# Fused norms, transposed weighted values and a bias moved to VectorE in an eight-stage transformer kernel

## The chip, the cores and the metric

One core of a Trainium2 chip runs the whole kernel. The time is device microseconds from start to end, the median of several runs; lower is better. Beside the runs there is one execution taken by the hardware profiler, from which all rows below come.

## What is computed

The reference keeps a residual `x` of 8 batches x 128 rows x 512 columns and passes it through four layers of an attention and a feed-forward network. Each of the eight adds its result, scaled by a gate, to the residual:

```python
x = x + jnp.tanh(g_xattn[l]) * attention_l(_layernorm(x), ctx)
x = x + jnp.tanh(g_ffn[l]) * ffn_l(_layernorm(x))
```

Five of them are touched by the change. The first feed-forward rounds its three weight matrices to the 16 levels of NF4 (blocks of 64, scaled by the block's largest value) and then computes `silu(x @ w1.T) * (x @ w2.T) @ w3.T`, with 1376 hidden columns. The second attention is a linear attention over the context. The second feed-forward mixes eight low-rank experts per batch:

```python
q = x.mean(axis=1) @ Wq.T                       # one query per batch
coeffs = softmax(q @ lora_keys.T / sqrt(128))   # 8 experts
h = einsum('bsi,eir->bser', x, lora_down)       # rank 64 each
out = x @ W_org.T + einsum('be,bser,ero->bso', coeffs, h, lora_up)
```

The third attention has 16 query heads of 96 columns that share 4 key and value heads, over 128 context and 128 own positions. The third feed-forward is `x @ W_base.T + b_base` and, per row, the two best of eight rank-16 experts.

## The kernel before

The residual stays in SBUF. The eight sublayers are stages, one Python function each: `l0_attention`, `l0_ffn`, `l1_attention`, `l1_ffn`, `l2_attention`, `l2_ffn`, `l3_attention`, `l3_ffn`.
**The norm.** Ahead of each sublayer `layernorm_all` (L108) is a block of its own. `row_stats` (L102) has taken the statistics of each batch when it was updated. The block then makes mean and variance of the 8 batches (DVE, L135 and L137), the reciprocal root by a power (POOL, L170), and normalises 8 batches on DVE (L152, L157 and L163). Where the sublayer wants it transposed, PE transposes each batch (L185, L194) into PSUM and ACT copies it out (L204) to `chip.hall`, which the stages call `h_t`. Only two buffers are there, so that DVE, PE and ACT take turns. The block can be given loads for SP to issue and work for POOL (`prepare`).

**`l0_ffn`** (L678). The weights come in 11 chunks. For each, DVE takes the largest values (L912), divides by them (L924), and compares with the 15 boundaries: each comparison is a `side`, 128x1536 in f16 (L932). PE sums the sides, each multiplied with a diagonal matrix that carries the step of its level (`level`, L776: three matmuls). The 15 diagonals are written by POOL at L737, in the norm's block. For chunk 0, PE waits for all of them at once. The main block follows, with the gate and up products (L795) and the down products (L847), and DVE's update of `x` (L979).

**`l1_attention`** (L1038). After its norm, SP issues here the loads for `l2_attention` (`l2_attention_loads`, L1015). The last is the output weight `wo`, one transfer of 3 MB.

**`l1_ffn`** (L1233). A loop over four pairs of batches. POOL copies a batch of `h_t` (L1278), PE makes the down products (L1290, 16 matmuls of 128 columns), the query (L1295) and the scores (L1301), DVE and ACT make the softmax, DVE scales the down products by it (`hl`), and PE sums base and up products (L1306, L1309, four matmuls of 512 columns each).

**`l2_attention`** (L1459). It runs batch by batch in one cycle, in which PE works for batch `b` and prepares `b + 1`:

```python
scores_t(b, 0); output(b - 1, range(6, OT)); scores_t(b, 1)     # PE, cycle(b), shortened
queries(n, 0); weighted_values(b, 0); queries(n, 1); weighted_values(b, 1)
queries(n, 2); weighted_values(b, 2); keys(n, 0); weighted_values(b, 3)
keys(n, 1); keys(n, 2); values(n, 0); o_transposed(b, 0); o_transposed(b, 1); scores(n, 0)
o_transposed(b, 2); values(n, 1); scores(n, 1); output(b, range(0, 3)); maxima_as_rows(n); output(b, range(3, 6))
```

`scores_t` (L1624, L1627) makes the scores transposed, in `a_ps_st`; ACT's `exponential` (L1732) turns them into probabilities, `a_p_t_ctx` and `a_p_t_lat`. `weighted_values(b, r)` (L1640) takes the 128x128 probabilities of one head as the stationary operand and 97 columns as the moving one: the 96 values and a column of ones, which gives the sum. DVE takes the reciprocal of the sums and multiplies (L1815, L1817), PE transposes the result (L1651), ACT copies it (L1737), and `output` (L1661) multiplies it with `wo` in 12 tiles. On DVE the same cycle rounds the weights of the last feed-forward (`rounding`).

**`l2_ffn`** (L1882). Pairs of batches again. Per batch PE sums four base matmuls (L1957), one that adds the bias (`ones` of 1x128 by the bias, L1958), a transpose (L1960) and the experts' product (L1962).

Of the kernel before, what the change touches and what calls it, by code (L numbers as in the profile page):

```python
# [16 lines left out]
ALU = mybir.AluOpType  # L17
# [3 lines left out]
P = 128  # L21
NB = 8
# [85 lines left out]
def layernorm_all(chip, tag, transposed, loads=None, rms=False, prepare=None, scratch=None):  # L108
# [103 lines left out]
    if transposed:  # L212
        chip.ln_counts["transposed"] += NB
        chip.ln_counts["stored"] += NB

# [462 lines left out]
def l0_ffn(chip):  # L678

    nc, a = chip.nc, chip.args
# [12 lines left out]
    with ExitStack() as ctx:  # L694
# [40 lines left out]
        def diagonals(pool):  # L735
            for k in range(LEVELS):
# [3 lines left out]
        layernorm_all(chip, "f0", transposed=True, loads=first_loads, prepare=diagonals,  # L740
                      scratch=q[:, :].rearrange("p (u n) -> p u n", u=2))
# [6 lines left out]
        with nc.Block() as block:  # L748
            @block.sync
            def _(sp):  # L750
                with sp.Fori(1, MT // 2) as i:
# [10 lines left out]
                sp.dma_start(wch[:, 0, 2 * D:2 * D + LAST3], w3[:, m * D:FLAT]).then_inc(s_wl[0], 16)  # L762

            @block.tensor
            def _(pe):
                pe.sem_inc(s_used, RING)
                pe.sem_inc(s_u, 2)
                pe.wait_ge(s_dg, LEVELS)

                def level(m, k, first=False):  # L770
                    after(pe, s_sg, m * LEVELS + (k + 1))
# [53 lines left out]

                for k in range(LEVELS):
                    level(0, k, first=True)
                transposed(0, 0, first=True)
                transposed(0, 1)
                step(0, 0)  # L830
# [21 lines left out]
            def _(act):  # L852
# [38 lines left out]

                w3_scaled(0, 0)
# [14 lines left out]
            def _(dve):  # L907
# [54 lines left out]

                maxima(0, 0, 48)
                normalized(0, 0, first=True)
                sides(0, 0, range(LEVELS))
# [11 lines left out]
                for b in range(NB):  # L977
# [3 lines left out]
                    row_stats(chip, dve, b, s_x, b + 1)  # L981

# [32 lines left out]
def l2_attention_loads(chip):  # L1015
# [12 lines left out]
    return loads + [(wv, a["l2_wv"], landed), (wo, a["l2_wo"], landed)]  # L1028
# [3 lines left out]
L2_LOADS = KT * U2 * (1 + HEADS2 // KV2) + 2  # L1032
# [5 lines left out]
def l1_attention(chip):  # L1038
# [3 lines left out]
    layernorm_all(chip, "a1", transposed=False, loads=l1_ffn_loads(chip))  # L1042
# [190 lines left out]
def l1_ffn(chip):  # L1233

# [3 lines left out]
    worg, down, up, wq, keys = l1_ffn_weights(chip)  # L1240
    with ExitStack() as ctx:
# [3 lines left out]
        psc, phl, pout = ps("ps_score", [P, 2, D]), ps("ps_hl", [P, 2, D]), ps("ps_out", [P, 2, D])  # L1245
        ones = sb("ones", [P, P])
        hs = sb("h_b", [P, 2, KT, P])
        hm = sb("h_sum", [P, 2, KT])
        qb = sb("q_bcast", [P, 2, P])
        nmx = sb("neg_max", [P, 2, 1])  # L1250
        e8 = sb("exp", [P, 2, E1])
        es = sb("exp_sum", [P, 2, 1])
        er = sb("exp_rec", [P, 2, 1])
        cc = sb("coeff", [P, 2, KT])
        hl = sb("hl", [P, 2, KT, P])
# [203 lines left out]
def l2_attention(chip):  # L1459
# [10 lines left out]
    with ExitStack() as ctx:  # L1470
# [69 lines left out]
        with nc.Block() as block:  # L1540
# [23 lines left out]
            def _(pe):  # L1564
# [66 lines left out]
                def weighted_values(b, r, first=False):  # L1631
                    if r == 0:
                        after(pe, s_v, b * 2 + 2)
# [1156 lines left out]
```

## Time and profile before

| what | value |
|---|---|
| median of 3 runs | 1694.49 us (1693.63 to 1696.26) |
| the profiled execution | 1687.38 us |
| its span, first to last instruction | 1685.6 us |
| its mean granted TensorE clock | 0.92 |
| PE busy | 1444.7 us (86%) |
| DVE busy | 1021.8 us (61%) |
| ACT busy | 356.8 us (21%) |
| POOL busy | 62.8 us (4%) |

The stages stand one behind the other, so the profile is read stage by stage: the time of a row is the start of an instruction or of a run of like instructions, counted from the start of the span, and the figure behind it is how long they took. A bracket says how long the engine had been idle and which operation ended the wait. The shares of the table are means over eight stages with different limits.

### The profile page before, as it was taken

Reading aid. Unit: us, or ns where it says so; the run is one execution under the profiler, and the core shown is the slowest. Engines: PE = TensorE matmul, PEld = TensorE weight load, DVE = VectorE, ACT = ScalarE, POOL = GpSimd, SP = SyncE. Lnnn points to the kernel's source line nnn. Section 1 sums busy time; section 2 is a strip of 40 time slices with the busy share of each in tenths; the row PEclk is TensorE's granted clock in tenths of the full one; section 3 lists DMA queues with packets and bytes.
Section 4 is the critical chain, followed back from the end, with each engine's and each line's share of the span. In section 5 each row is a group of like instructions: output and inputs, shape, how many; then the busy total and the mean of one; then the engine's idle time right before and its main releaser. Section 6 shows DMA issues by size and latency. Waiting matters only on the chain. (4 is left out here: it accounts for less than half of the span.)

```text
span 1685.6 us, 26597 instructions
## 1 busy us (share of the span) xinstructions
PE 1444.7 (86%) x8875; PEld 891.3 (53%) x8875; DVE 1021.8 (61%) x1652; ACT 356.8 (21%) x705; POOL 62.8 (4%) x100
## 2 busy tenths in 40 slices
PE   2989758999999966997999999999787789996575
PEld 1666623444444435665667777666443656652232
DVE  6577569778871137233566667666334256767886
ACT  1333321111113012101112121211111223332221
POOL 2000020000000000000000000000004000000000
PEclk9999858999999988898999999999698899998887
DMA  5000011011100037000000000000120000000000
GB/s 208 2 0 0 1 38 38 20 38 37 33 0 1 0 98 171 0 0 6 27 22 18 21 26 26 20 26 21 66 40 1 1 1 1 0 0 1 12 19 19
DMA packets 52311, 44.56 MB, mean 26 GB/s; under 512 B 38497, under 2 KB 38689, under 8 KB 51362
## 3 DMA queue, kind: packets, MB, share of 16 engines
q1 hardware_dynamic: 52258, 43.85, 8.8%
q8 instruction: 33, 0.54, 0.1%
q14 instruction: 20, 0.16, 0.0%
HBM read 41.74 MB, written 2.10 MB: 26 GB/s over the span
## 5 line engine op out<-in xcount | busy, mean ns | idle before, releaser
L932 DVE TENSOR_SCALAR f_side<-f_chunk 128x1536 f16<-128x1536 f32 x165 | 148.1, 955 | 46.1 <-PE f_sum L776 45.0
L776 PE MATMUL f_sum<-f_side,f_diag 128*128 128x512 f16 x495 | 122.2, 389 | 9.6 <-DVE f_side L932 8.1
L776 PEld LDWEIGHTS f_sum<-f_side,f_diag 128*128 128x128 f16 x495 | 47.9, 100 | 92.0 <-issue 45.0
L1573 PE MATMUL a_ps_b<-h_all,weights_a 128*128 (+1 forms) x768 | 92.1, 280 | 1.3 <-PEq L124 1.3
L1573 PEld LDWEIGHTS a_ps_b<-h_all,weights_a 128*128 128x128 f32 x768 | 89.1, 195 | 5.9 <-issue 5.9
L1661 PE MATMUL a_ps_y<-weights_a,a_o_t 128*128 128x512 f32 x192 | 89.3, 613 | 2.7 <-DVE a_v_ones L1793 2.0
L795 PE MATMUL f_gate<-h_all,f_w_t 128*128 128x512 f32 (+1 forms) x176 | 87.6, 598 | 0.0
L795 PE MATMUL f_up<-h_all,f_w_t 128*128 128x512 f32 (+1 forms) x176 | 79.6, 592 | 0.0
L847 PE MATMUL f_sum<-weights_a 128*128 128x512 f32 (+1 forms) x176 | 75.7, 592 | 0.0
L453 PE MATMUL a_o<-weights_a 128*128 128x128 f32 x512 | 70.1, 287 | 0.0
L453 PEld LDWEIGHTS a_o<-weights_a 128*128 128x128 f32 x512 | 62.7, 196 | 7.4 <-issue 3.5
L2237 PE MATMUL a_ps_a<-h_all,weights_a 128*128 (+1 forms) x512 | 64.1, 286 | 2.5 <-DVE a_sel L2482 2.5
L2237 PEld LDWEIGHTS a_ps_a<-h_all,weights_a 128*128 128x128 f32 x512 | 61.3, 200 | 9.2 <-issue 9.2
L2508 DVE TENSOR_REDUCE a_neg_max<-a_ps_a 128x8 f32<-128x1024 f32 x32 | 39.2, 1225 | 37.2 <-PE a_ps_a L2267 37.2
L1661 PEld LDWEIGHTS a_ps_y<-weights_a,a_o_t 128*128 128x128 f32 x192 | 35.6, 195 | 46.1 <-issue 45.9
L598 DVE TENSOR_REDUCE a_neg_max<-a_sa 128x8 f32<-128x1024 f32 x32 | 39.2, 1225 | 34.3 <-PE a_sa L416 34.0
L389 PE MATMUL a_proj<-h_all,a_wqk 128*128 (+1 forms) x64 | 36.6, 685 | 25.6 <-DVE a_neg_lo L564 24.1
L847 PEld LDWEIGHTS f_sum<-weights_a 128*128 128x128 f32 (+1 forms) x176 | 33.4, 190 | 42.2 <-issue 42.2
L1640 PE MATMUL a_ps_o<-a_v_ones,a_p_t_ctx 128*128 128x97 f32 x256 | 51.6, 285 | 4.0 <-DVE a_o L1817 3.2
L2416 ACT ACTIVATE a_p_t<-a_ps_st 128x512 f32<-128x512 f32 x64 | 34.8, 596 | 87.7 <-PE a_ps_st L2293 87.6
L170 POOL TENSOR_TENSOR ln_rstd<-ln_meanvar,ln_minus_half 128x8 f32<-128x8 f32 x7 | 11.6, 1652 | 1095.2 <-DVE ln_meanvar L137 1095.2
L795 PEld LDWEIGHTS f_up<-h_all,f_w_t 128*128 128x128 f32 (+1 forms) x176 | 32.8, 188 | 37.0 <-issue 35.6
(334 smaller groups left out, 2677.1 us busy)
## 6 DMA issues: line engine op xcount, KB each, us to landing
f_chunk<-in_l_w SPq DMA_DIRECT2D x30, 256.0 KB, 3.0
weights_a<-in_l_wgu SPq DMA_DIRECT2D x16, 232.0 KB
weights_a<-in_l_wq SPq DMA_DIRECT2D x48, 64.0 KB, 2.4
weights_a<-in_l_wo SPq DMA_DIRECT2D x1, 3072.0 KB, 11.6
weights_a<-in_l_wd SPq DMA_DIRECT2D x16, 192.0 KB, 3.1
x_res<-in_x SPq DMA_DIRECT2D x1, 2048.0 KB, 8.1
ctx_nat<-in_ctx SPq DMA_DIRECT2D x1, 2048.0 KB, 11.2
a_mask<-in_mask SPq DMA_DIRECT2D x1, 2048.0 KB, 15.7
```

The source lines that it names most:

```text
L389: nc.tensor.matmul(pproj[:, g % 2, :], wqk[:, g, :], h_n[:, bass.ds(b, 1), :].rearrange("p a n -> p (a n)"), start=True, stop=True).then_i ...
L453: mm = nc.tensor.matmul(po[:, c], vpad[:, s, n, k * P:(k + 1) * P], pt[:, k % 4, c], start=(k == 0 and n == 0), stop=(k == H0 - 1), skip_g ...
L598: nc.vector.tensor_reduce(to, psa[:, :, :].rearrange("p e (n j) -> p e n j", n=WN), AX.X, ALU.max, negate=True).then_inc(s_max, 1)
L776: mm = nc.tensor.matmul(psum[:, j, :], diag[:, k, :], side[:, k % RING, j * D:(j + 1) * D], start=(k == 0), stop=(k == LEVELS - 1), skip_g ...
L795: mm = nc.tensor.matmul((pg, pu)[w][0:r, g, :], wt[:, u, w, k, 0:r], h_t[:, k, g * D:(g + 1) * D], start=(k == 0), stop=(k == KT - 1), ski ...
L847: mm = nc.tensor.matmul(psum[:, i % 2, :], hid[0:r, t, i * P:(i + 1) * P], w3t[0:r, t, :], start=(t == 0), stop=(t == MT - 1))
L932: nc.vector.tensor_scalar(side[:, k % RING, :], wch[:, u, :], bounds[k], steps[k][0], ALU.is_le if k < ZERO else ALU.is_gt, ALU.mult).then ...
L1573: mm = nc.tensor.matmul(pb[:, u % 2, g * P:(g + 1) * P], wq_of(k, u, g), h_t[:, k, bass.ds(b * P, P)], start=(k == 0), stop=(k == KT - 1))
L1640: mm = nc.tensor.matmul(po[:, g * (HD2 + 1):(g + 1) * (HD2 + 1)], p, v[:, part, r, :], start=(part == 0), stop=(part == 1))
L1661: mm = nc.tensor.matmul(py[:, :], ot[:, t, :], wo[:, t, :], start=(t == 0), stop=(t == OT - 1))
L2237: mm = nc.tensor.matmul(pa[:, u // QG, (u % QG) * P:(u % QG + 1) * P], wq[:, k, u * P:(u + 1) * P], hb(b)(k), start=(k == 0), stop=(k == K ...
L2508: nc.vector.tensor_reduce(to, pa[:, :, :].rearrange("p e (i j) -> p e i j", i=QG), AX.X, ALU.max, negate=True).then_inc(s_max, 1)
```

## The change

A new class, `NextNorm`, takes the place of several norm blocks. Its parts are mean, variance (DVE), the power (POOL, for one batch) and the normalising pass (DVE), and a stage calls them batch by batch.

**A. `l0_ffn`.** Its norm block is gone. The norm's first parts stand ahead of chunk 0's maxima on DVE; six of eight normalising passes stand between the first sides. PE transposes each batch between the levels, into the banks of the gate product, and ACT copies it. Each level of chunk 0 waits for its own diagonal. At the end of the stage DVE normalises each batch for `l1_attention` behind its update. The five loads of `l1_ffn`'s weights are issued in this stage.

```diff
-        layernorm_all(chip, "f0", transposed=True, loads=first_loads, prepare=diagonals,
-                      scratch=q[:, :].rearrange("p (u n) -> p u n", u=2))
+        first_norm = NextNorm(chip, sem, "first")
...
+            @block.gpsimd
+            def _(pool):
+                pool.wait_ge(first_norm.s_mv, 2 * NB)
+                nc.gpsimd.tensor_tensor(chip.ln_rstd[:], chip.ln_mv[:, :, 1], chip.ln_mhalf[:], ALU.pow)\
+                  .then_inc(first_norm.s_rstd, NB)
+                diagonals(pool)
+                for b in range(NB):
+                    norm.rstd(pool, b)
...
                 def level(m, k, first=False):
+                    if first:
+                        pe.wait_ge(s_dg, k + 1)
...
+                first_norm.meanvars(dve)
+                for b in range(2):
+                    input_normalized(b)
                 maxima(0, 0, 48)
                 normalized(0, 0, first=True)
-                sides(0, 0, range(LEVELS))
+                for k in range(LEVELS):
+                    sides(0, 0, range(k, k + 1))
+                    if k < NB - 2:
+                        input_normalized(k + 2)
...
                     row_stats(chip, dve, b, s_x, b + 1)
+                    norm.meanvar(dve, b)
+                    norm.normalized(dve, b, chip.hall[:, b * D:(b + 1) * D])
```

On PE, at the start of `l0_ffn`, the order before was this (`ln_psf` is the norm's PSUM, `f_diag` the diagonals):

```order
L185 MATMUL ln_psf<-ident,f_q 128x128 x8
L188 UNCONDITIONAL_BRANCH
L188 ISA
L32 REGISTER_ALU
L194 MATMUL ln_psf<-ident,f_q 128x128 x4
L32 REGISTER_ALU
L194 MATMUL ln_psf<-ident,f_q 128x128 x4
L188 REGISTER_ALU
L188 COMPARE_AND_BRANCH
L124 UNCONDITIONAL_BRANCH
L764 UNCONDITIONAL_BRANCH
L776 MATMUL f_sum<-f_side,f_diag 128x512 x45
```

Now the same place on PE reads:

```order
L831 MATMUL f_gate<-ident,f_q 128x128 x8
L843 MATMUL f_sum<-f_side,f_diag 128x512 x3
L831 MATMUL f_gate<-ident,f_q 128x128 x4
L843 MATMUL f_sum<-f_side,f_diag 128x512 x3
L831 MATMUL f_gate<-ident,f_q 128x128 x4
L843 MATMUL f_sum<-f_side,f_diag 128x512 x3
```

This alternates until six transposed batches stand between seven levels; the other eight levels follow, and no block ends in between.

**B. `l1_attention`.** Its norm block is gone, and `wo` is laid out anew, in 16 transfers:

```diff
-    layernorm_all(chip, "a1", transposed=False, loads=l1_ffn_loads(chip))
...
-    return loads + [(wv, a["l2_wv"], landed), (wo, a["l2_wo"], landed)]
+    for r in range(KV2):
+        for m in range(4):
...
+            loads.append((to[:, m], a["l2_wo"][32 * m:32 * m + 32, U2 * r:U2 * r + U2, :], landed))
```

**C. `l1_ffn`.** Its own norm block stays, the loop over pairs is written out straight. The down products take 512 columns at a time (four batches). Queries, scores and softmax are made once for all batches. POOL's copies are gone. Behind each update DVE normalises the batch for `l2_attention`, and PE transposes it after the next batch's output:

```diff
+                downs(0, (0, 1))
+                queries()
+                downs(0, (2,))
+                scores()
+                downs(0, (3,))
...
+                for b in range(NB):
+                    if b == HALF:
+                        downs(1, range(KT))
+                    outputs(b)
+                    if b:
+                        transposed(b - 1)
+                transposed(NB - 1)
```

**D. `l2_attention`.** Its norm block is gone. The weighted values turn round: 32 columns of ones or of values are stationary, in four column groups beside one another (one for each key head), and 512 columns of probabilities move. The result comes out transposed, so PE's 12 transposes and ACT's copies are gone. DVE takes one reciprocal of 128x512 and multiplies three times:

```diff
+                    for out, of in [(po, lambda part, r: ones32[:, :])] + \
+                            [(pst[:, u, :], lambda part, r, u=u: v[:, part, r, 32 * u:32 * u + 32]) for u in range(U)]:
+                        for part, p in enumerate((pt0, pt1)):
+                            for r in range(KV2):
+                                mm = nc.tensor.matmul(out[row(r), :], of(part, r), p[:, r, :], start=(part == 0),
+                                                      stop=(part == 1), skip_group_check=True)
...
+                def reciprocals(b):
+                    after(dve, s_pv, b * 4 + 1)
+                    nc.vector.reciprocal(rec[:, :], po[:, :]).then_inc(s_rec, 1)
...
-                            weighted_values(b, r)
-                        o_transposed(b, 0, (s_ot, b * 3))
-                        o_transposed(b, 1)
-                        o_transposed(b, 2, (s_ot, b * 3 + 1))
+                        weighted_values(b)
                         output(b, range(OT), (s_x, b))
```

On PE, in a cycle of `l2_attention`, the place of the weighted values before (two of the four heads groups; `a_ps_b` from `h_all` are the queries of the next batch):

```order
L1573 MATMUL a_ps_b<-h_all,weights_a 128x128 x16
L1640 MATMUL a_ps_o<-a_v_ones,a_p_t_ctx 128x97
L1640 MATMUL a_ps_o<-a_v_ones,a_p_t_lat 128x97
L1640 MATMUL a_ps_o<-a_v_ones,a_p_t_ctx 128x97
L1640 MATMUL a_ps_o<-a_v_ones,a_p_t_lat 128x97
L1640 MATMUL a_ps_o<-a_v_ones,a_p_t_ctx 128x97
L1640 MATMUL a_ps_o<-a_v_ones,a_p_t_lat 128x97
L1640 MATMUL a_ps_o<-a_v_ones,a_p_t_ctx 128x97
L1640 MATMUL a_ps_o<-a_v_ones,a_p_t_lat 128x97
L1573 MATMUL a_ps_b<-h_all,weights_a 128x128 x16
```

Now:

```order
L1708 MATMUL a_ps_b<-h_all,weights_a 128x128 x16
L1777 MATMUL a_ps_o<-a_p_t_ctx,a_ones 32x512 x4
L1777 MATMUL a_ps_o<-a_p_t_lat,a_ones 32x512 x4
L1777 MATMUL a_ps_st<-a_p_t_ctx,a_v 32x512 x4
L1777 MATMUL a_ps_st<-a_p_t_lat,a_v 32x512 x4
L1777 MATMUL a_ps_st<-a_p_t_ctx,a_v 32x512 x4
L1777 MATMUL a_ps_st<-a_p_t_lat,a_v 32x512 x4
L1777 MATMUL a_ps_st<-a_p_t_ctx,a_v 32x512 x4
L1777 MATMUL a_ps_st<-a_p_t_lat,a_v 32x512 x4
L1708 MATMUL a_ps_b<-h_all,weights_a 128x128 x16
L1726 MATMUL a_ps_y<-weights_a,a_ctx_b 128x384 x4
```

All weighted values of a batch stand together, after the first queries of the next; its first values (`a_ctx_b`) come earlier. All four ACT buffers of `a_p_t_lat` are there, so no exponential waits for PE to free one. The outputs are cut 0 to 2, 3 to 5, 6 and 7, and 8 to 11 (before: 0 to 2, 3 to 5, 6 to 11); the scores of the next batch wait for the three multiplications, since they write the same PSUM.

**E. `l2_ffn`.** The bias matmul is gone. The bias is loaded to all 128 partitions, scaled by the gate once, and added to `x` on DVE ahead of each batch's update:

```diff
-                        nc.tensor.matmul(pout[:, u, :], ones[:, :], bias, start=False, stop=False)
...
+                        nc.vector.tensor_tensor(chip.x_at(b), chip.x_at(b), bias, ALU.add).then_inc(s_xb, 1)
+                    for u in range(2):
+                        b = pair * 2 + u
+                        after(dve, s_xb, b + 1)
```

## Rows read from the trace of the kernel before

**Rows 1.** Windows, a cycle and the end of `l2_attention`: us; busy by engine; clock; DMA

```profile
core 0: us, PE busy (x) PEld busy (x) DVE busy (x) ACT busy (x) POOL busy (x), PEclk, DMA share, GB/s
971.00:1019.50 48.50, 48.17 (x368) 35.15 (x364) 33.26 (x63) 9.90 (x19) 0.00 (x0) 1.00 0.08 23
1177.00:1198.00 21.00, 15.46 (x80) 13.79 (x76) 13.89 (x29) 4.04 (x7) 0.00 (x0) 0.63 0.00 1
```

**Rows 2.** Timeline, start of `l0_ffn`, DVE, POOL and the SP queue: start, duration

```profile
234.24 2.70 SPq L129 DMA_DIRECT2D f_chunk<-in_l_w  x6
...
236.90 1.08 DVE L157 TENSOR_SCALAR f_q<-x_res,ln_meanvar,ln_rstd 128x512 f32<-128x512 f32 x2 [1.77 <-POOL ln_rstd L170]
...
236.96 10.35 POOL L737 TENSOR_SCALAR f_diag<-ident 128x128 f16<-128x128 f32 x15
...
247.76 1.75 DVE L912 TENSOR_REDUCE f_absmax<-f_chunk 128x24 f32<-128x1536 f32 x1 [2.67 <-PEq L124]
...
251.90 2.70 DVE L932 TENSOR_SCALAR f_side<-f_chunk 128x1536 f16<-128x1536 f32 x3
```

**Rows 3.** Tile `f_chunk`, the six chunk transfers, 230 to 262 us

```profile
DMA to landing us min/median/max: 2.7/4.3/5.3
```

**Rows 4.** Timeline, `l0_ffn`'s end into `l1_attention`, DVE and the SP queue

```profile
614.74 0.75 DVE L979 SCALAR_TENSOR_TENSOR x_res<-f_sum,tanh_g,x_res 128x512 f32<-128x512 f32 x1 [7.97 <-PE f_sum L847]
...
624.75 0.39 SPq L1080 DMA_DIRECT2D weights_a<-in_l_wk  x1
...
658.66 0.43 SPq L1080 DMA_DIRECT2D weights_a<-in_l_wo  x1
...
668.03 0.69 DVE L105 BATCH_NORM_STATS2 ln_stats<-x_res 128x6 f32<-128x512 f32 x1
```

**Rows 5.** Lines by form, POOL's power for one batch, elsewhere: busy, mean ns

```profile
L2118 POOL TENSOR_TENSOR ln_rstd<-ln_meanvar,ln_minus_half 128x1 f32 x8 | 4.4, 544 | 229.8 <-DVE ln_meanvar L2112 229.8
```

**Rows 6.** Timeline, `l1_ffn` and the start of `l2_attention`, POOL and PE

```profile
683.16 0.20 POOL L1273 MEMSET f_ones<- 128x128 f32 x1 [11.06 <-POOLq L124]
...
773.44 3.60 PE L1306 MATMUL f_ps_out<-weights_b,f_h_b 128*128 128x512 f32 x8
776.88 3.60 PE L1309 MATMUL f_ps_out<-weights_b,f_hl 128*128 128x512 f32 x8
...
796.53 3.76 PE L1573 MATMUL a_ps_b<-h_all,weights_a 128*128 128x128 f32 x17 [1.25 <-PEq L124]
```

**Rows 7.** Timeline, PE, one cycle of `l2_attention`, 1017 to 1069 us

```profile
1034.51 0.36 PE L1640 MATMUL a_ps_o<-a_v_ones,a_p_t_ctx 128*128 128x97 f32 x2
...
1036.27 3.76 PE L1573 MATMUL a_ps_b<-h_all,weights_a 128*128 x32
...
1056.75 1.04 PE L1651 MATMUL a_ps_b<-ident,a_o 128*128 128x128 f32 x8
...
1058.48 0.66 PE L1651 MATMUL a_ps_b<-ident,a_o 128*128 128x128 f32 x4
...
1062.82 2.81 PE L1661 MATMUL a_ps_y<-weights_a,a_o_t 128*128 128x512 f32 x6 [0.33 <-DVE a_v_ones L1793]
```

**Rows 8.** Timeline, ACT, the same cycle, its first four exponentials

```profile
1022.66 2.06 ACT L1732 ACTIVATE a_p_t_ctx<-a_ps_st 128x512 f32<-128x512 f32 x4 [11.58 <-PE a_ps_st L1627]
```

**Rows 9.** Timeline, PE, `l3_attention`: 128x32 column groups of 512 columns

```profile
1400.87 1.06 PE L2304 MATMUL a_ps_o<-a_p_t,a_v_pad 128*32 128x512 f32 x8
1401.75 1.04 PE L2304 MATMUL a_ps_den<-a_p_t,a_ones 128*32 128x512 f32 x8
```

**Rows 10.** Lines by form, DVE's reciprocal of 128x512 in `l3_attention`

```profile
L2520 DVE RECIPROCAL a_rec<-a_ps_den 128x512 f32<-128x512 f32 x8 | 26.8, 3356 | 2.9 <-PE a_ps_den L2304 2.9
```

**Rows 11.** Timeline, PE, the last cycle of `l2_attention`

```profile
1165.77 2.86 PE L1624 MATMUL a_ps_st<-a_q_t,a_k_t 32*128 32x512 f32 x24
...
1198.08 12.88 PE L1661 MATMUL a_ps_y<-weights_a,a_o_t 128*128 128x512 f32 x24 [0.77 <-ACT a_o_t L1737]
```

**Rows 12.** Timeline, PE, `l2_ffn`, around one bias matmul

```profile
1251.59 1.12 PE L1958 MATMUL f_ps_out<-f_bias,f_ones 1*128 1x512 f32 x2
1252.64 0.33 PE L1960 MATMUL f_ps_tr<-ident,f_weighted 128*128 128x128 f32 x1
```

More of the change, by code:

```diff
@@ L1273, in _ @@
                 nc.gpsimd.memset(ones[:], 1.0).then_inc(s_c, 1)
-                with pool.Fori(0, NB // 2) as pair:
-                    for u in range(2):
-                        b = pair * 2 + u
-                        after(pool, s_y, b + 1)
-                        nc.gpsimd.tensor_copy(hs[:, u, :, :], h_t[:, :, bass.ds(b * P, P)]).then_inc(s_hs, 1)
+                for b in range(NB):
+                    norm.rstd(pool, b)
             @block.tensor
@@ new lines, in _, with downs @@
+                pe.wait_ge(s_c, 1)
+                def downs(part, tiles):
+                    if part and tiles[0] == 0:
+                        pe.wait_ge(s_hl, HALF)
+                    for t in tiles:
+                        for k in range(KT):
+                            mm = nc.tensor.matmul(phl[:, t, :], down[:, k, t * P:(t + 1) * P],
+                                                  h_t[:, k, part * D:(part + 1) * D], start=(k == 0), stop=(k == KT - 1))
+                        mm.then_inc(s_hp, 1)
@@ new lines, in queries, with scores @@
+                def queries():
+                    pe.wait_ge(s_hm, 1)
+                    for k in range(KT):
+                        mm = nc.tensor.matmul(pq, wq[:, k, :], hm[:, k, :], start=(k == 0), stop=(k == KT - 1))
+                    mm.then_inc(s_q, 1)
+                def scores():
+                    pe.wait_ge(s_qk, 1)
+                    nc.tensor.matmul(pscore, ones[:], qk[:, :, :].rearrange("p b e -> p (b e)"), start=True, stop=True)\
+                      .then_inc(s_sc, 1)
@@ L1313, in _ @@
+                for b in range(NB):
+                    if b == HALF:
+                        downs(1, range(KT))
+                    outputs(b)
+                    if b:
+                        transposed(b - 1)
+                transposed(NB - 1)
             @block.scalar
             def _(act):
[L1315 to L1320 removed]
+                act.wait_ge(s_sh, 1)
@@ L1364 @@
+                for part in range(2):
+                    for b in range(part * HALF, part * HALF + HALF):
+                        scaled(b)
+                    for b in range(part * HALF, part * HALF + HALF):
+                        updated(b)
 MXB = 32
@@ L1561, in _ @@
                         raw_loads(j, p)
+            @block.gpsimd
+            def _(pool):
+                constants(pool)
             @block.tensor
```

393 lines of the change are left out of this document (212 added, 181 removed).

## The prediction

> **What bounds the kernel now.** I read the shares first, then windows by stage, since a share over eight stages says nothing of one, and then the timelines at the places that the diff touches. In `l2_attention` PE is the bound: in a window of 48.50 us, about one cycle, it is busy for 48.17 at full granted clock, and DVE for 33.26 [rows 1]. So what PE no longer does there comes off the time, as long as DVE, which gets more, stays below. At the two ends of a stage it is otherwise: there the chain is norm, barrier, first product, and every engine but one waits. At the start of `l0_ffn` DVE makes its first maximum at 247.76, after a norm and 2.67 us of waiting for the block's end [rows 2]. Between `l0_ffn`'s last update at 614.74 and the first load of the next stage at 624.75 lie 10 us of norm and barriers [rows 4], between `l1_ffn`'s last product (776.88 + 3.60 = 780.48) and the first queries 16.05 [rows 6]. The last cycle of `l2_attention` has no next batch to cover its waits: it lasts from 1165.77 to 1198.08 + 12.88 = 1210.96, 45.2 us, with a granted clock of 0.63 in the middle [rows 1, 11].
>
> The sum is made against the profiled execution, 1687.4 us, which lies 7.1 under the median of 1694.5; I take the same difference off the median.
>
> **A, the first feed-forward: 4.0.** Before, sides begin at 251.90, which is 4.14 after the maxima begin [rows 2]. Now the maxima need two normalising passes, which ended at 236.90 + 1.08 = 237.98, and the chunk. Its third transfer is issued by about 235.6 (half of six that take 2.70 from 234.24) and lands 4.3 later [rows 2, 3], at 239.9. Sides can begin at 244.0, 7.9 earlier. Against it stand the six other passes, 6 x 0.55 = 3.3 on DVE, which paces the levels here. Transposes by PE and copies by ACT lie beside sides of 0.9 us each. For a slow first stretch of PE I take off another 0.6; 4.0 remain. The diagonals do not hold the levels: they come every 10.35 / 15 = 0.69 from 236.96 on [rows 2], and a side takes longer. Bounds: 6.4, if the chunk lands with the second pass and nothing else is lost. Below, DVE and POOL may get in each other's way: with sides from 244.0 there are some 5 diagonals left, and with the passes and maxima ahead of them up to 10, at 0.69 each; that would make it -3. But two passes took 1.08 while diagonals were being written, so I stay with 4.0.
>
> The Trainium skill (SBUF — State Buffer, "SBUF: two separate sides") speaks against this part: VectorE and GpSimd share a port pair that one operation holds alone, and the other blocks until it is done. By that, the 10 diagonals would cost up to 6.9 and A would come out below nothing; the two passes beside diagonals, 0.54 each [rows 2], don't show such a block.
>
> **B, the second attention's norm: 5.8.** The last update starts at 614.74 and takes 0.75. Behind it now come statistics (0.69, [rows 4]), mean and root's argument (some 0.3 with their waits), POOL's power (0.54, [rows 5]) and one pass (0.55): with the waits between them 618.0, and with a barrier of 0.9, 618.9 instead of 624.75. Bounds 4.7 to 6.0. SP gets 15 more issues of 0.43 for `wo`, 6.5 in all. Their cover: the old last one ends at 659.09, and the stage's last update has its statistics until 668.72 [rows 4], so 9.6 us are free. They would cost if an issue took over 0.64.
>
> **C, the second feed-forward: 17.8.** Four matmuls of 512 columns take 3.44 from start to start, 0.86 each [rows 6]. PE now has 32 for the down products (27.5) and 64 for the outputs (55.0), small products of 1.2, and seven times four transposes at 0.12 to 0.13 (3.6); for a slow start I add 1.5. From 683.4, when the block starts [rows 6], that is 88.8 and ends at 772.2, 8.3 earlier. DVE's work for a batch (scaling, update, norm: about 3.5) hides behind 6.9 of output; if it did not, each of six batches would pay the rest. Of the end, 16.05 before, there stay update, norm (3.5 as in B without its barrier), four transposes at half clock and a copy (2.0) and the barrier (0.9): 6.4, so 9.6 less. I take 17.8 for both; bounds 14 (if softmax delays the first outputs by its whole chain) and 19.
>
> **D, the third attention: 22.3.** Per cycle goes 4 x 1.76 = 7.04 of weighted values (1034.51 to 1036.27 for one of four), 12 transposes of 1.04 + 0.66 busy, about 1.5 without overlap, and the wait of 0.33 [rows 7]. There come 8 groups of four matmuls. `l3_attention` has the same form: one to the next takes 1401.75 - 1400.87 = 0.88 [rows 9], so 7.04. Left are 1.8, of which I keep 1.5 for changes of operand and tiling: 7 cycles, 10.5. The new wait is for DVE: reciprocal 3.36 [rows 10] and three multiplications of 0.7 take the place of four small pairs, 2.5 more in 33.3 of 48.5. By its order they are done some 22 us into a cycle, and PE needs them at about 38, after the queries, keys and values of the next batch. Bounds 0 (the wait takes all) and 12.6.
>
> The last cycle now is: transposed scores and four output tiles, 3.0 + 3.6 + 3.0; four exponentials that nothing covers, 2.06 [rows 8] and 0.3; 7.1 of weighted values, behind which the reciprocal hides; 1.0 for the last multiplication; 12 output tiles, 12.88 as before [rows 11]. That is 33.0, 12.2 less. Bounds: 14.4 at full clock throughout. With the clock at half from the exponentials on, 14.2 and 21.4 replace 7.1 and 12.88: 48.6, a loss of 3.4. I take 12.2, since PE has one wait of 2.4 now where it had one before each of four groups. POOL's constants, no longer beside a norm, cost 0.4 at the start.
>
> The Trainium skill (TensorEngine Tiling (Array Packing), "Key Properties") says that a change of tiling mode drains TensorE. Its cost is bounded by a row: a group of 1.06, followed after 0.88 [rows 9], leaves at most 0.18 hidden, twice a batch, 2.9 in all.
>
> **E, the third feed-forward's bias: 7.6.** From the bias matmul to the next instruction are 1.05 [rows 12]; eight are 8.4. I take 0.95 each, since a transpose that follows another row of products may start a little dearer. DVE gets 0.69 per batch, ahead of an update that waits for PE. Bounds 8.4, and 0 if DVE ends each pair.
>
> **Sum:** 4.0 + 5.8 + 17.8 + 22.3 + 7.6 = 57.5. The profiled execution would take 1629.9, the median 1637.0.
>
> **The rivals.** *Tilings drain* (0.10): each batch enters and leaves the column groups, at 0.18 each: 1640. For it: the group's 1.06 against 0.88; against it: the next group, without a change, shows 1.04 too. The skill's page on tiling has this rule.
>
> *The first norm does not hide* (0.12): what the change says of A does not come about; passes between the sides delay PE's levels as much as the norm did, A is 0, and 1641. For it: DVE paces this stretch, and the passes are on it still. Against: the wait of 2.67 and the ping-pong of DVE, PE and ACT are gone in any case.
>
> *DVE ends the cycle* (0.08): reciprocal and rounding push the maxima of the next batch behind PE, and the 10.5 of the steady cycles go: 1647.5. For it: the maxima already stand close ahead of PE's last tiles, which waited 0.33 for DVE [rows 7]. Against: 15 us of DVE's cycle are free.
>
> *Half clock in the last cycle* (0.10): 12.2 turns into -3.4, and 1652.6. For it: the granted clock was 0.63 between 1177 and 1198 [rows 1], after waits of PE; against: fewer waits.
>
> *The other side, slower* (0.02): the four column groups run one behind another. A group of four then takes 4 x 0.88 = 3.5, 2.64 more, 64 times: 169, and 1806. It decides from 57.5 / 64 = 0.9 more per group, about 1.8, on. Against it: 0.88 in `l3_attention` for the same form [rows 9]. Only that operands sit elsewhere speaks for it.
>
> **How the numbers follow.** The forecast has 0.58. A measurement of this kernel can tell about 0.2%, 3.4 us, from no change; all cases but the last are over 30 us faster, so faster has 0.97, slower 0.02, and 0.01 is for several bounds met at once. Downwards the bounds of A, C, D and E reach 57.5 + 2.4 + 1.2 + 4.3 + 0.8, 1628; with 2.6 for the scatter of the runs, 1625. Upwards the range takes in all rivals but the last: 1652.
>
> **What would show it.** In the changed kernel sides of chunk 0 should begin near 244, and the gate product some 4 us earlier against that stage's start. `l0_ffn`'s last update should be followed by the next stage's first load within 4.2. `l1_ffn` should last some 89 us and the next stage's queries follow its last product by 6 to 7. A group of four at the weighted values should take 0.88; the transposed scores of the next batch should follow after 47.2 or so, and PE should not wait for the multiplications. The last cycle should last 33. Groups over 1.0, a wait of PE for DVE in the cycle, or a granted clock near 0.6 over the last outputs would prove the sum wrong.

## The result, and the profile after

| what | before | changed |
|---|---|---|
| median of 3 runs | 1694.49 us | 1632.45 us (1631.99 to 1637.58) |
| ratio, 95% interval | | 0.9641 [0.961, 0.9673] |
| the profiled execution, its span | 1687.38, 1685.6 | 1637.58, 1635.9 |

The forecast was 1637.0 between 1625 and 1652, by 57.5 us. The medians differ by 62.0, the profiled executions by 49.8, and a second measurement, further down, gives a ratio of 0.9685 [0.9653, 0.9718], 52.9 us. So the totals alone can't judge a sum of 57.5. The stages can. I cut both traces at the same events: the statistics that begin a norm, the second maximum of `l0_ffn`, the last update and the first load behind it, the first and the last product of a stage.

| stretch | before | changed | less by | forecast |
|---|---|---|---|---|
| start to `l0_ffn`'s statistics (`l0_attention`) | 234.28 | 241.28 | -7.0 | 0 |
| A: to chunk 1's maxima | 31.45 | 26.48 | 5.0 | 4.0 |
| the other chunks, to the last update | 349.01 | 347.42 | 1.6 | 0 |
| B: to the next stage's first load | 10.01 | 3.99 | 6.0 | 5.8 |
| `l1_attention` | 44.78 | 47.04 | -2.3 | 0 |
| `l1_ffn`'s norm block | 13.63 | 12.89 | 0.7 | 0 |
| C: `l1_ffn`'s body and the way to the next queries | 97.32 + 16.05 | 88.40 + 5.89 | 19.1 | 17.8 |
| D: `l2_attention` | 414.43 | 393.08 | 21.4 | 22.3 |
| E: `l2_ffn`, to the next norm's statistics | 82.57 | 76.65 | 5.9 | 7.6 |
| the rest | 392.07 | 392.78 | -0.7 | 0 |

The five parts give 57.4 together. What the profiled executions differ from that lies in stretches for which the sum had nothing, above all in the first, which has no edit. The windows view of the changed kernel shows it (us, busy time by engine, granted clock, DMA); in the kernel before the same window has a granted clock of 0.87.

```profile
20.00:60.00 40.00, 28.68 (x199) 16.99 (x200) 20.64 (x41) 9.77 (x16) 0.00 (x0) 0.74 0.15 58
941.00:988.00 47.00, 46.72 (x353) 28.66 (x351) 35.36 (x59) 8.02 (x16) 0.00 (x0) 1.00 0.08 23
1130.00:1166.00 36.00, 32.88 (x189) 13.15 (x187) 30.46 (x50) 4.13 (x8) 0.00 (x0) 1.00 0.07 18
```

The second and third line are a cycle and the last cycle of `l2_attention`, to set beside [rows 1]: PE is still the bound, DVE has 35.36 instead of 33.26, and the last cycle now runs at full granted clock.

**A and B.** The timeline of the changed kernel at `l0_ffn`'s start and end, DVE, POOL and the SP queue (start, duration; beside [rows 2] and [rows 4]):

```profile
241.15 2.70 SPq L795 DMA_DIRECT2D f_chunk<-in_l_w  x6
...
241.28 0.64 DVE L239 BATCH_NORM_AGGREGATE ln_meanvar<-ln_stats 128x2 f32<-128x6 f32 x8 [1.00 <-PEq L87]
...
244.11 15.60 POOL L777 TENSOR_SCALAR f_diag<-ident 128x128 f16<-128x128 f32 x15
...
247.28 1.75 DVE L988 TENSOR_REDUCE f_absmax<-f_chunk 128x24 f32<-128x1536 f32 x1 [2.14 <-DMA f_chunk<-in_l_w]
...
251.40 0.96 DVE L1008 TENSOR_SCALAR f_side<-f_chunk 128x1536 f16<-128x1536 f32 x1
252.28 0.54 DVE L252 TENSOR_SCALAR f_q<-x_res,ln_meanvar,ln_rstd 128x512 f32<-128x512 f32 x1
252.74 1.04 DVE L1008 TENSOR_SCALAR f_side<-f_chunk 128x1536 f16<-128x1536 f32 x1
...
267.76 1.74 DVE L988 TENSOR_REDUCE f_absmax<-f_chunk 128x24 f32<-128x1536 f32 x1
...
615.18 0.75 DVE L1066 SCALAR_TENSOR_TENSOR x_res<-f_sum,tanh_g,x_res 128x512 f32<-128x512 f32 x1 [6.35 <-PE f_sum L919]
...
619.17 0.38 SPq L1173 DMA_DIRECT2D weights_a<-in_l_wk  x1
```

The maxima wait for the chunk, as the sum had it. Sides begin 10.12 after the statistics, 7.5 earlier than before (7.9 forecast). A pass between two sides costs 0.46 from start to start, not 0.55. The diagonals take 15.60 instead of 10.35, but not evenly. The same row in three parts, with DVE's division of the chunk:

```profile
244.11 5.66 POOL L777 TENSOR_SCALAR f_diag<-ident 128x128 f16<-128x128 f32 x9
249.61 1.76 DVE L1000 TENSOR_TENSOR f_chunk<-f_chunk,f_rec 128x1536 f32<-128x1536 f32 x1
249.85 2.65 POOL L777 TENSOR_SCALAR f_diag<-ident 128x128 f16<-128x128 f32 x1
252.59 7.13 POOL L777 TENSOR_SCALAR f_diag<-ident 128x128 f16<-128x128 f32 x5
```

Nine diagonals come every 0.64. The tenth starts beside the division and takes 2.65. The last five stand beside sides and come every 1.4, as often as a side with its pass.

**C and D.** PE in the changed kernel: the end of `l1_ffn` (beside [rows 6]), then one cycle of `l2_attention` (beside [rows 7]) and the last one (beside [rows 11]).

```profile
763.90 3.60 PE L1410 MATMUL f_ps_out<-weights_b,f_hl 128*128 128x512 f32 x8
...
770.75 0.66 PE L1425 MATMUL f_ps_norm<-ident,f_next_h 128*128 128x128 f32 x4 [2.82 <-DVE f_next_h L252]
773.39 13.32 PE L1708 MATMUL a_ps_b<-h_all,weights_a 128*128 128x128 f32 x96 [1.98 <-POOL a_ones L1664]
...
945.30 2.86 PE L1759 MATMUL a_ps_st<-a_q_t,a_k_t 32*128 32x512 f32 x24
...
958.71 1.06 PE L1777 MATMUL a_ps_o<-a_p_t_ctx,a_ones 128*32 128x512 f32 x8
959.59 1.04 PE L1777 MATMUL a_ps_o<-a_p_t_lat,a_ones 128*32 128x512 f32 x8
960.45 1.04 PE L1777 MATMUL a_ps_st<-a_p_t_ctx,a_v 128*32 128x512 f32 x8
...
964.74 1.04 PE L1777 MATMUL a_ps_st<-a_p_t_lat,a_v 128*32 128x512 f32 x8
965.71 3.84 PE L1708 MATMUL a_ps_b<-h_all,weights_a 128*128 x32
...
984.65 2.81 PE L1788 MATMUL a_ps_y<-weights_a,a_o_t 128*128 128x512 f32 x6 [0.24 <-DVE a_v L1898]
987.39 0.83 PE L1741 MATMUL a_ps_st<-a_k,a_q 32*128 32x256 bf16 x24
988.16 2.84 PE L1788 MATMUL a_ps_y<-weights_a,a_o_t 128*128 128x512 f32 x6
...
991.18 1.88 PE L1788 MATMUL a_ps_y<-weights_a,a_o_t 128*128 128x512 f32 x4
992.99 2.86 PE L1759 MATMUL a_ps_st<-a_q_t,a_k_t 32*128 32x512 f32 x24
...
1136.07 2.86 PE L1759 MATMUL a_ps_st<-a_q_t,a_k_t 32*128 32x512 f32 x24
...
1147.96 1.07 PE L1777 MATMUL a_ps_o<-a_p_t_ctx,a_ones 128*32 128x512 f32 x8 [2.18 <-issue]
...
1155.93 10.54 PE L1788 MATMUL a_ps_y<-weights_a,a_o_t 128*128 128x512 f32 x24 [0.90 <-DVE a_o_t L1925]
```

A group of four column groups takes 0.86, as long as a single matmul of 512 columns ([rows 6], 3.44 for four), so they run beside one another. A cycle is 992.99 - 945.30 = 47.69; before, three cycles took 146.28 (from 1019.48 to the last one's 1165.77), 48.76 each. The last cycle takes 1166.47 - 1136.07 = 30.4 instead of 45.2.

**E.** The changed kernel in `l2_ffn`, from all engines (beside [rows 12]):

```profile
1172.00 8.55 SPq L129 DMA_DIRECT2D weights_a<-in_l_wv  x1
...
1186.79 3.96 PE L2066 MATMUL f_ps_ra<-f_w_ra,f_h_b 128*128 128x136 f32 x16 [5.29 <-POOL f_h_b L2053]
...
1201.31 2.34 PE L2066 MATMUL f_ps_ra<-f_w_ra,f_h_b 128*128 128x136 f32 x16
1203.48 3.60 PE L2073 MATMUL f_ps_out<-f_w_base,f_h_b 128*128 128x512 f32 x8
1206.92 0.27 PE L2075 MATMUL f_ps_tr<-ident,f_weighted 128*128 128x128 f32 x1
1207.72 1.10 PE L2077 MATMUL f_ps_out<-f_w_b,f_weighted_t 128*128 128x512 f32 x2 [0.53 <-ACT f_weighted_t L2089]
...
1213.83 2.34 PE L2066 MATMUL f_ps_ra<-f_w_ra,f_h_b 128*128 128x136 f32 x16
...
1227.36 14.95 POOL L2186 TENSOR_SCALAR weights_a<-f_raw_queries,weights_a 128x256 f32<-128x256 f32 x16
...
1239.35 0.75 DVE L2140 SCALAR_TENSOR_TENSOR x_res<-f_ps_out,tanh_g,x_res 128x512 f32 x1 [1.56 <-PE f_ps_out L2077]
...
1243.12 0.64 DVE L135 BATCH_NORM_AGGREGATE ln_meanvar<-ln_stats 128x2 f32<-128x6 f32 x8 [2.08 <-PEq L87]
```

A pair of batches takes 1213.83 - 1201.31 = 12.52; before it took 14.92, so a batch is 1.20 shorter. Beside the bias matmul of [rows 12] stood, before:

```profile
1248.07 3.60 PE L1957 MATMUL f_ps_out<-f_w_base,f_h_b 128*128 128x512 f32 x8
...
1253.50 1.10 PE L1962 MATMUL f_ps_out<-f_w_b,f_weighted_t 128*128 128x512 f32 x2 [0.53 <-ACT f_weighted_t L1974]
```

So 1.05 of the 1.20 is the matmul itself; the base products ahead of it took 3.52 and take 3.44 now, and the transpose took 0.86 to the next product and takes 0.80. From the first product to the last update that is 52.56 instead of 62.05, so 9.5 less. But the first product comes 2.3 later after the norm's statistics than before, and from the last update to the next statistics pass 3.77 instead of 2.47: POOL works until 1242.31.

### The profile page after: what moved, and what is told of

It reads as the page before. It is cut to its first block and busy times, and to the rows that moved or that the text cites. A ratio compares the mean times of both kernels' runs of the same rounds, so it can differ in the third digit from the quotient of the medians.

```text
span 1635.9 us, 25134 instructions
## 1 busy us (share of the span) xinstructions
PE 1409.3 (86%) x8501; PEld 811.8 (50%) x8501; DVE 1042.4 (64%) x1603; ACT 338.8 (21%) x666; POOL 69.3 (4%) x105
## 5 line engine op out<-in xcount | busy, mean ns | idle before, releaser
L492 PE MATMUL a_o<-weights_a 128*128 128x128 f32 x512 | 74.6, 300 | 0.0
L492 PEld LDWEIGHTS a_o<-weights_a 128*128 128x128 f32 x512 | 67.1, 208 | 8.1 <-issue 4.5
L1759 PE MATMUL a_ps_st<-a_q_t,a_k_t 32*128 32x512 f32 x384 | 48.7, 623 | 1.6 <-DVE a_neg_max_block L1912 0.8
L1906 DVE TENSOR_REDUCE a_neg_max<-a_ps_st 128x4 f32<-128x1024 f32 x32 | 37.7, 1220 | 12.0 <-PE a_ps_st L1741 12.0
```

The costliest lines, as they stand in the source:

```text
L492: mm = nc.tensor.matmul(po[:, c], vpad[:, s, n, k * P:(k + 1) * P], pt[:, k % 4, c], start=(k == 0 and n == 0), stop=(k == H0 - 1), skip_g ...
L1759: nc.tensor.matmul(pst[:, r, :], kt[row(r), u, part * P:(part + 1) * P], qt[row(r), u, :], start=(u == 0), stop=False, skip_group_check=True)
```

## The experiments

**The parts, one at a time.** Four runs undo one part of the changed kernel and keep the others: A (norm and diagonals in a block of their own again), B, C, D; a fifth undoes E. Their edits are the diffs of the change, read backwards (C's run also makes the third attention's norm a block again, D's loads `wo` in one transfer again); of each the line that stands for it, shortened:

```diff
+        layernorm_all(chip, "f0", transposed=True, loads=first_loads, prepare=diagonals,
+                      scratch=q[:, :].rearrange("p (u n) -> p u n", u=2))
```

> The changed kernel with the first feed-forward's norm as a block of its own ahead of chunk 0, with POOL's diagonals in it; the rest as changed. Theory (part A is worth what the stage shows, 4.97): chunk 1's maxima begin 31.45 after the stage's first statistics instead of 26.48, and 1637.4 in all. Rival (the moved norm gave nothing, and the stage's earlier end came from later chunks): the maxima come as early, 1632.4.

```diff
-                    norm.normalized(dve, b, chip.hall[:, b * D:(b + 1) * D])
...
+    layernorm_all(chip, "a1", transposed=False)
```

> The changed kernel with the second attention's norm as a block again; the 16 transfers of the output weight stay. Theory (part B is worth 6.0): from the first feed-forward's last update to the next stage's first load 10.0 instead of 4.0, 1638.4 in all. Rival (the 16 transfers cost what the norm gives: the second attention took 2.3 longer in the changed kernel): then the stage from its first load to the next norm's statistics stays at 47.0 here too, and it is the 16 transfers that make it so; if it falls to 44.8 in this run or differs from run to run, it is the granted clock.

```diff
-                downs(0, (0, 1))
-                queries()
...
+                        nc.gpsimd.tensor_copy(hs[:, u, :, :], h_t[:, :, bass.ds(b * P, P)]).then_inc(s_hs, 1)
...
+        layernorm_all(chip, "a2", transposed=True, prepare=constants, scratch=ot[:, 0:2, :])
```

> The changed kernel with the second feed-forward as before (pairs of batches, POOL's copies, 128 columns) and with the third attention's norm as a block. Theory (part C is worth 19.1: 8.9 in the products, 10.2 at the end): from the stage's first memset to its last product 97.3 instead of 88.4, from there to the next queries 16.05 instead of 5.9, and 1651.5 in all. Rival (the 512-column products alone matter, the norm at the end hides elsewhere): 9 us, 1641.

```diff
-                        weighted_values(b)
+                        for r in range(KV2):
+                            weighted_values(b, r)
+                        o_transposed(b, 0, (s_ot, b * 3))
```

> The changed kernel with the third attention's products as before (97 columns move, transposes, four small reciprocals per batch, the output weight in one transfer); its norm stays with the second feed-forward. Theory (part D is worth the 21.35 that the stage shows: 7 cycles of 1.07, and 14.8 in the last one): a cycle of 48.76, the last one 45.2 with a granted clock of 0.6 in it, 1653.8 in all. Rival (half of the last cycle's 14.8 was the clock that one execution happened to have): the last cycle 33 to 38 and 1643 to 1647.

```diff
+                        nc.tensor.matmul(pout[:, u, :], ones[:, :], bias, start=False, stop=False)
```

> The changed kernel with the third feed-forward as it was before: the bias is a matmul again and one 2 KB transfer. Theory (the part is worth what the stage shows: products 9.5 us shorter, but 1.8 given back while SP issues the stage's loads, and 1.3 while POOL finishes): from the last update of the third attention to the statistics of the next norm 82.5 instead of 76.6, and 1638.4 us in all. Rival (PE's sum alone counts, the waits at both ends of the stage are chance of one execution): 9.5 longer, 1642. Both say that SP's issue of the values' weights takes 6.9 again, not 8.55, if it is the bias's 128 copies that hold it up; if it stays at 8.5, the copies have nothing to do with it.

| part undone | its stretch, changed | in this run | worth | all, median (4 runs) |
|---|---|---|---|---|
| A | 26.48 | 32.29 | 5.8 | 1641.31 |
| B | 3.99 | 10.53 | 6.5 | 1640.65 |
| C | 88.40 + 5.89 | 97.51 + 15.92 | 19.1 | 1650.14 |
| D | 393.08 | 415.05 | 22.0 | 1661.33 |
| E | 76.65 | 82.22 | 5.6 | 1641.96 |

Each stretch returns to within 0.9 of what it was before, so each gain belongs to its part, and the rivals fall; the sum is 59.0. How far a stretch scatters by itself is seen in the traces that leave its part in place: A's is 25.0 to 26.5 in nine traces, B's 3.95 to 3.99 in ten, C's 92.6 to 94.9 and D's 393.1 to 395.6 in ten (the longest is the run that undoes C), E's 76.4 to 77.3 in seven. A's scatters because the first maxima begin 4.1 to 6.0 after the statistics, with the landing of the chunk, and the later chunks make up for it: from the statistics to the stage's last update the nine take 373.5 to 374.6, the run that undoes A 380.1, the kernel before 380.5. Over the stage A is worth 5.5 to 6.6.

The medians of all lie 1.4 to 7.5 us off the totals that the theories gave, too much to read a part of 6 from them. E's median, 9.5 above the changed kernel's, would have spoken for the rival; by its ratio to the kernel before, 0.9701 against 0.9641 and 0.9685, E reads as anything from 3 to 10. D's last cycle takes 45.42 again, and the windows view of that run shows the clock of its middle:

```profile
1155.00:1176.00 21.00, 15.13 (x84) 13.36 (x76) 14.00 (x29) 4.00 (x7) 0.00 (x0) 0.64 0.00 1
```

So the low clock returns with the old order of waits, and is a part of D's worth. In the run without B, with the 16 transfers, `l1_attention` took 47.5; in the run without D, with one transfer, 47.1; in the runs without A, C and E 45.9 to 46.1. Neither the transfers nor the norm set it. It goes with the granted clock of the stage: 0.79 in the six traces with 47.0 to 47.5, 0.80 to 0.82 in the five with 45.9 to 46.1, 0.83 in the kernel before, with 44.8. E's run also shows SP's issue of the values' weights without the bias's 128 copies ahead of it:

```profile
1163.57 6.96 SPq L129 DMA_DIRECT2D weights_a<-in_l_wv  x1
```

**The wait for the diagonals.** One line:

```diff
-                        pe.wait_ge(s_dg, k + 1)
+                        pe.wait_ge(s_dg, LEVELS)
```

> The changed kernel, where each level of chunk 0 waits for all 15 diagonals, as before. Theory (POOL writes a diagonal in 1.04 now instead of 0.69, since DVE works beside it, and is done 18.4 us after the stage's statistics begin, 8 us behind the first side; the three side buffers then stop DVE): the maxima of chunk 1 come 3 to 5 later than 26.5 us after the start, and 1636 in all, so most of what the moved norm gained hangs on the wait being cut up. Rival (DVE's stop lets POOL finish sooner and PE catches up, since its levels are shorter than DVE's sides): under 1 us, 1633.

Chunk 1's maxima came 31.66 after the statistics instead of 26.48, and 1640.22 in all. The whole gain of A goes, 5.2 where 3 to 5 were expected. The timeline, POOL, PE and DVE:

```profile
239.00 13.01 POOL L777 TENSOR_SCALAR f_diag<-ident 128x128 f16<-128x128 f32 x15
...
252.06 1.46 PE L843 MATMUL f_sum<-f_side,f_diag 128*128 128x512 f16 x3 [10.47 <-POOL f_diag L777]
...
254.42 0.55 DVE L252 TENSOR_SCALAR f_q<-x_res,ln_meanvar,ln_rstd 128x512 f32<-128x512 f32 x1 [4.98 <-PE f_gate L831]
```

DVE stops for 4.98, though not for a side's buffer as expected: its next pass waits for a transpose that stands behind the first level in PE's order.

**The bias's place.** The transfer is issued last, with a semaphore of its own:

```diff
+            + [(bias, chip.args["l2_bias"].rearrange("a n -> (a n)").partition_broadcast(P), s_bias)])
...
-                dve.wait_ge(chip.s_l2f, 16 * 4)
+                dve.wait_ge(s_bias, 16)
```

> The changed kernel with the bias's transfer issued behind all others of that block, on a semaphore of its own, so that the products don't wait for it. Theory (the 128 copies ahead of the values' weights hold SP's issues up, and the block ends with SP): the values' weights are issued in about 6.9 instead of 8.55, the stage's first product comes about 1.7 earlier after the norm's statistics, 1630.7 in all. Rival (SP's long issue is paced by the transfers of the values' weights themselves): 8.5 stays, and no change, 1632.4.

SP's long issue fell to 7.18 and the norm block ended 1.5 earlier. But the stage took 77.85, not less than 76.65, and 1632.01 in all. The timeline shows the wait that took its place, which neither theory had:

```profile
1167.23 7.18 SPq L129 DMA_DIRECT2D weights_a<-in_l_wv  x1
...
1178.91 0.42 SPq L129 DMA_DIRECT2D f_bias<-in_l_bias  x1
...
1185.54 0.49 DVE L2098 TENSOR_SCALAR f_bias<-f_bias,tanh_g 128x512 f32<-128x512 f32 x1 [5.42 <-DMA f_bias<-in_l_bias]
...
1189.72 0.30 PE L2076 MATMUL f_ps_tr<-ident,f_weighted 128*128 128x128 f32 x1 [1.83 <-DVE f_weighted L2128]
```

DVE scales the bias ahead of all its work, so it waited for the transfer, and PE for DVE.

**Three ends of stages.** As the run before, with POOL's layout of the next queries cut in four portions and PE's waits for POOL's constants put ahead of their first use.

```diff
-                l3_queries_laid_out(chip, pool, raw_queries)
+                    l3_queries_laid_out(chip, pool, raw_queries, pair)
...
                 pe.wait_ge(chip.s_l2a, 16 * L2_LOADS)
-                pe.wait_ge(s_c, 3)
...
                 values(0, 0)
+                pe.wait_ge(s_c, 3)
                 scores(0, 0)
```

> As the run with the bias last, and two more: POOL lays out the next attention's queries in four portions between its copies instead of behind the last (14.95 us that end 1.3 after DVE), and PE waits for POOL's constants only ahead of their first use (it waited 1.40 for ones in the second feed-forward and 1.98 for ones in the third attention, of which part is the barrier). Theory (the stage ends with POOL, and the starts with POOL's constants): the third feed-forward ends 1.3 earlier, the two starts 0.3 to 0.8 each earlier; with the bias's 1.7 some 4 in all, 1628.4. Rival (the portions delay the copies that PE needs, and the block's barrier was the wait at the starts): the copies come up to 2 late per pair, no gain in all, 1631 or more.

The portions did what they should: 2.48 from the last update to the next statistics instead of 3.77, and 76.52 for the stage, with the bias's wait still in it. The constants gave nothing: the queries began 0.5 earlier after the last product (5.37), and `l2_attention` took 0.6 longer (393.68). In all 1633.39 (6 runs), no change.

**The loads later.** The bias stays in its place; SP issues the fourth attention's loads in the main block, POOL's portions follow the copies from the second pair on.

```diff
-            + l3_attention_loads(chip, raw_queries))
...
+            @block.sync
+            def _(sp):
+                for dst, src, landed in l3_attention_loads(chip, raw_queries):
+                    sp.dma_start(dst, src).then_inc(landed, 16)
```

> The changed kernel, where SP issues the fourth attention's loads in the third feed-forward's main block instead of its norm block (the bias stays where the change has it), and POOL lays out the queries in four portions behind its copies from the second pair on. Theory (the norm block ends with SP's issues, 3 us behind the last copy of the norm, and the main block with POOL, 1.3 behind DVE): the stage's first memset comes 2.3 earlier after the norm's statistics (14.2 instead of 16.5), the next norm's statistics 1.3 earlier after the last update, the stage takes 73.0 instead of 76.65, 1628.8 in all. Rival (the loads then land too late for POOL, or their transfers hold up the products): 76 or more, and no change in all.

> The changed kernel itself once more, beside the run with the loads later. Theory (its stages after the first are the same from run to run, and the first attention takes 234 to 241 with no edit in it, by the granted clock of its first part: 0.87 against 0.74 between 20 and 60 us): stages within 1 of those of the first profile, apart from the first attention, the second (45.9 to 47.5) and the part behind the third feed-forward (390 to 398); a time from 1629 to 1638. Rival (the new code itself sets the slower clock at the start): 241 here too, and in every other run that has the changed first feed-forward; four of those runs have shown 235 to 237.

On the same chip, six runs each: 1629.08 (1625.22 to 1634.12) with the loads later, 1633.98 (1631.23 to 1637.46) for the changed kernel; against the kernel before 0.9662 [0.9627, 0.9698] and 0.9685 [0.9653, 0.9718]. The intervals overlap; the stretch does not leave it in doubt: 71.63 with the loads later, 76.64 for the changed kernel again (76.4 to 77.3 in seven traces), so 5.0 where 3.6 were expected. From the norm's statistics to the main block's first memset pass 13.7 instead of 16.5, and the rest of the stage is 2.2 shorter. The SP queue and POOL in that run:

```profile
1177.19 5.00 SPq L2047 DMA_DIRECT2D weights_a<-in_l_wv  x1
...
1217.19 7.24 POOL L2193 TENSOR_SCALAR weights_a<-f_raw_queries,weights_a 128x256 f32<-128x256 f32 x8
...
1232.60 1.67 POOL L170 TENSOR_TENSOR ln_rstd<-ln_meanvar,ln_minus_half 128x8 f32<-128x8 f32 x1 [8.17 <-DVE ln_meanvar L137]
```

POOL is done 8 us ahead of the next norm. Of the kernels tried it has the lowest median.

The changed kernel's second profile agrees with the first within 0.1 in B, C, D and E. `l0_attention`, which no run edits, took 241.2 to 241.6 in five of the eleven traces of the changed kernel and its variants, with a granted clock of 0.74 between 20 and 60 us, and 234.6 to 237.3 in the other six, with 0.83 to 0.87. The same code takes both, so the rival falls, and the 7 us are not the new code's cost. Whether it meets the lower clock more often than the kernel before, of which there is one trace, is not shown.

## Why the prediction was right

The forecast of 1637 lies 4.6 above the median; the sum of 57.5 meets 57.4 in the stages. That both are so close is in part luck: the profiled execution was to take 1629.9 and took 1637.6, and inside D two errors cancel. Of the terms:

**A** was 4.0 and is 5.0, or 5.8 against the run that undoes it alone. The landing of the chunk was near: maxima 6.0 after the statistics, 5.6 forecast. The passes were priced too high (0.46 from start to start), and the 0.6 for a slow start of PE was not needed. The rival that the norm does not hide is wrong, but only through the wait by level: without it A is worth 0.6, by the two undoing runs (31.66 and 32.29). The prediction said that the diagonals do not hold the levels, from 0.69 each. The reason was wrong: beside the sides they come every 1.4, no faster than side and pass together, 1.42. The sentence came true because ten of the 15 are written when the first level starts (252.50), and because each level waits for its own alone.

The Trainium skill's rule on the port pair (SBUF — State Buffer, "SBUF: two separate sides") bears on this. For VectorE it names operations in a mode that uses both port pairs, or with two operands in SBUF, a condition that the prediction left out when it set the two passes against the rule. The trace agrees with a block: a diagonal takes 0.53 while DVE waits or takes maxima, 2.65 when it starts beside the division, which has two operands in SBUF, 1.34 beside the sides, and 0.53 again in the run with the one wait for all, while DVE stands still. But POOL is the one that pays, 15.60 - 10.35 = 5.3. Sides take 1.04 instead of 0.95 and passes stay at 0.54, so the loss of A that could be worked out from the rule did not come. By the page the operation that starts first has the pair; here POOL's diagonal starts at 252.59 and the side at 252.74, and POOL waits all the same.

**B** was 5.8 and is 6.0; the 16 transfers were hidden, as the runs with and without them show. **C** was 17.8 and is 19.1: 8.9 for 8.3 in the products, 10.2 for 9.6 at the end.

**D** was 22.3 and is 21.4, with two errors that cancel. The steady cycle was to gain 1.5 and gained 1.07, the first of the seven 0.8, in all 7.2 instead of 10.5. By the two traces, 12 output tiles in four pieces take 11.06 where 10.66 were needed in three, the three rounds of queries take 0.15 more, and of the wait of 0.33 for DVE's copy of the values 0.24 stays; the prediction had 0.3 for all such changes. The rival that DVE ends the cycle holds at most for these tenths, not for the 10.5. The start of the stage lost 0.6, not 0.4. The last cycle was to gain 12.2 and gained 14.8: its outputs took 10.5, not 12.88, as the granted clock stayed up.

The Trainium skill's rule that a change of tiling drains TensorE (TensorEngine Tiling (Array Packing), "Key Properties") can have cost little here: the first group took 0.88 and the last one with the change back 0.97, where the others take 0.86, so 0.13 per batch, 1.0 in all, against a bound of 2.9. Whether that is the drain, no row shows.

**E** was 7.6 and is 5.9: a mis-sized term. The products gained 9.5, or 1.20 per batch instead of 0.95: without the bias matmul its neighbours are a little faster, not slower, as the step assumed. What the step missed is that both ends of the stage belong to other queues. SP's issues ended the norm block, which became 2.3 longer, 2.0 of it by the run without the bias's copies; POOL's layout of the next queries ended the main block, and a shorter block left it 1.3 behind. The prediction asked only whether DVE hides its addition.

**The slower side** fell with the first rows: 0.86 per group of four.

## What to carry to other kernels

When a stage gets shorter, ask which queue ends its block: a chain of DMA issues or a helper's loop that was hidden before may now be the end, and moving it can be worth almost as much as the edit itself (5.0 here, for an edit of 5.6 to 5.9). When a producer is moved beside a consumer, wait for each piece: the same move was worth 5.8 with a wait for each diagonal and 0.6 with one for all. Judge parts of a few us by stretches between equal events in several traces, since totals scatter more, and set the last event far enough behind that a late start is made up for. Read no cost from the mean of a merged row: 15.60 for 15 diagonals is 1.04 each, but they came every 0.64, took 2.65 once, and then came every 1.4.

## What the runs showed of the hardware

The granted clock in the last cycle of `l2_attention` goes with the order of the waits, though not without exception. With the old order PE waits 0.8 to 1.4 us ahead of each group of short products, and twice more behind them. The clock falls to its half level, 1.2 GHz (0.50 from 1186 to 1198 in the kernel before), and the mean over the middle is 0.63 and 0.64 in two traces; the 12 outputs behind it take 12.9 and 13.1. With the new order, one wait of 2.2 ahead of the products and one of 0.9 behind them, it stays at 2.4 GHz in nine traces of ten, and the outputs take 10.5. I had priced them as before. The tenth trace is the run without C, where the clock fell for a short time behind the same wait:

```profile
1160.00:1165.00 5.00, 3.27 (x20) 1.17 (x24) 3.85 (x10) 1.63 (x4) 0.00 (x0) 0.73 0.14 42
1161.72 1.48 PE L1734 MATMUL a_ps_o<-a_p_t_ctx,a_ones 128*32 128x512 f32 x8 [2.18 <-issue]
```

The first groups were slower, the outputs were at full clock again, and the last cycle took 32.1 instead of 30.4. What made the difference is not shown.

A transfer that spreads 2 KB to 128 partitions lands 5.4 to 7.4 us after its issue begins in eight traces where it is issued fourth, and 6.6 and 6.8 in the two where it is issued last. So it is no slower for being last (1178.91 to 1185.54 above); it only starts later. And SP's issue of one and the same transfer took 6.9 to 7.6 in four traces with no spread bias ahead of it, 8.4 to 9.6 in the seven with the bias three issues ahead, and 5.0 in the run that issues it a block later, 13 us behind the bias.
